# Edge loop of a graph kernel: source row buffers, the search for duplicates, and one head moved to VectorE

## The reference, cut to what matters

```python
x1 = x[edges[0]]
x2 = x[edges[1]]
e = jnp.concatenate([x1, x2], axis=1) @ Ww + bw
e = e.reshape(-1, H, 2 * HD).transpose(1, 0, 2)
e = jax.nn.leaky_relu(e, 0.01)
w = (e @ Wa + ba)[..., 0]
mat = jnp.full((H, n, n), -jnp.inf, jnp.float32)
mat = mat.at[:, edges[0], edges[1]].set(w)
mat = jax.nn.softmax(mat, axis=-1)
```

## Time and profile before

| | us |
|---|---|
| median of 3 runs | 837.27 |
| the runs' lowest and highest | 835.45, 837.58 |
| the profiled execution | 833.88 |
| its span in the trace | 832.2 |
| edge loop, from POOL's first destination gather to the last scatter's landing | 62.99 to 257.96 |

### The profile page before, as it was taken

How to read it: one execution, slowest core, us unless ns; L and a number is a source line. 1 busy time by engine, 2 the same in 40 slices (tenths; PEclk the granted TensorE clock), 3 DMA queues, 4 the chain that set the end, 5 groups by cost and what they waited for, 6 DMA issues and landing times.

```text
span 832.2 us, 9774 instructions
## 1 busy us (share of the span) xinstructions
PE 651.6 (78%) x2958; PEld 310.5 (37%) x2981; DVE 524.8 (63%) x1471; ACT 274.0 (33%) x1106; POOL 201.6 (24%) x223
## 2 busy tenths in 40 slices
PE   5972345622334929998989999989999999999997
PEld 2430112311113924455455545443434344343432
DVE  3377999989887996547473244764458745454533
ACT  2104675655661431446141010122222222222222
POOL 6047677777762000000000000011110101010100
PEclk9995556765555978999999999999999999999999
DMA  8588878788875619504000002569999999999981
GB/s 329 244 306 308 301 253 262 250 262 264 260 234 221 219 64 421 197 1 152 0 1 1 0 0 76 210 258 406 420 403 410 419 405 410 411 414 409 413 347 40
DMA packets 46648, 208.10 MB, mean 250 GB/s; under 512 B 7970, under 2 KB 12578, under 8 KB 37121
## 3 DMA queue, kind: packets, MB, share of 16 engines
q1 hardware_dynamic: 27296, 145.70, 44.1%
q0 software_dynamic: 19296, 61.75, 22.1%
HBM read 199.67 MB, written 10.31 MB: 252 GB/s over the span
## 4 chain that ended last, share of the span: by engine, by line
PE 59%; DVE 15%; DMA 9%; POOL 7%; issue 6%; ACT 2%; SPq 0%; DVEq 0%; POOLq 0%
PE bank L846 12%; PE bank L536 8%; PE bank L884 7%; PE bank L866 6%; PE bank L734 4%; PE bank L749 4%; DMA R<-tok_tab,slot_tok 3%; POOL R L447 3%; DVE R L1319 3%; POOL R L440 2%; PE bank L643 2%; PE bank L650 2%; DVE R L1323 2%; DMA score<-late,e_i 2%; PE bank L835 2%
## 5 line engine op out<-in xcount | busy, mean ns | idle before, releaser
L985 ACT ACTIVATE R<-R 128x128 f32<-128x128 f32 x384 | 113.0, 295 | 99.4 <-DVE R L1323 99.4
L584 PE MATMUL bank<-R 128*128 128x384 bf16 x144 | 49.7, 481 | 117.3 <-DVE R L1282 117.3
L846 PE MATMUL bank<-R 128*64 128x512 f32 (+1 forms) x432 | 105.9, 598 | 1.0 <-DVE R L1712 0.5
L489 POOL DMA_INDIRECT R<-tok_tab,slot_tok x33 | 33.0, 1000 | 261.7 <-DVE slot_f L1706 216.2
L536 PE MATMUL bank<-R,late 128*128 128x512 f32 x168 | 81.2, 646 | 0.7 <-DMA R<-L_Ww 0.7
L985 ACT ACTIVATION_READ_ACCUMULATOR R<-R 128x1 f32 x384 | 71.6, 187 | 0.0
L1319 DVE TENSOR_TENSOR R<-R 128x1032 f32<-128x1032 f32 x48 | 59.0, 1230 | 16.8 <-DMA R<-tab_src,e_i 9.2
L584 PEld LDWEIGHTS bank<-R 128*128 128x128 bf16 x144 | 13.4, 119 | 148.9 <-DVE R L1282 139.8
L1718 DVE TENSOR_TENSOR R<-R,bank 128x256 f32<-128x256 f32 x34 | 14.3, 420 | 86.7 <-ACT R L1098 86.7
L884 PE MATMUL bank<-R 128*128 128x512 bf16 x275 | 66.4, 380 | 2.5 <-issue 1.9
L478 POOL MEMSET R<- 128x512 f32 x3 | 1.6, 524 | 242.2 <-DVEq L1637 242.1
(11 more groups left out here) (376 smaller groups left out, 1133.8 us busy)
## 6 DMA issues: line engine op xcount, KB each, us to landing
R<-L_w SPq DMA_DIRECT2D x54, 1536.0 KB, 11.3
late<-L_w SPq DMA_DIRECT2D x18, 1536.0 KB, 10.2
R<-L_w SPq DMA_DIRECT2D x2, 3072.0 KB, 15.3
score<-R POOLq DMA_DIRECT2D x9, 512.0 KB, 12.5
R<-L_Ww SPq DMA_DIRECT2D x2, 2048.0 KB, 13.0
R<-L_W SPq DMA_DIRECT2D x4, 1024.0 KB, 9.0
R<-score SPq DMA_DIRECT2D x2, 1536.0 KB, 10.9
tab_src<-R SPq DMA_DIRECT2D x3, 516.0 KB, 2.7
```

The source lines that it names most:

```text
L584: last = pe.matmul(pb[s][:, 0:N], oh[:, e % 2, 0, P * s:P * s + P], oh[:, e % 2, 1, :], start=(e == 0), stop=(e == ET - 1))
L846: last = pe.matmul(pb[4 + i % 2][part, :], xeT[i % 2][:, k, part], w13[e % NWB][:, k, :], start=(k == 0), stop=(k == KD - 1), tile_positio ...
L985: act_.activation(own, own, ACT.Copy, accum_out=w_e3[:, t, h:h + 1]).then_inc(S("heads_summed"), 1)
```

## The change

1. `NGF` goes from 13 to 18. The five new buffers lie in `late0` and `late1`. Thirteen source gathers are still issued ahead of the loop (`NFRONT`); those of tiles 13 to 17 are issued in the loop at t = 0 to 4 and wait for no add, and from tile 18 on (t = 14) the loop gathers the source row of t+4 as before.
2. The search for duplicates compares each tile with the tile before it and with nothing else: one instruction of 128 values for each tile, none for tile 0. `tri` is gone. A duplicate inside one tile is written twice, with the same score.
3. In every odd tile VectorE's ReLU covers seven heads (896 values), and a further VectorE instruction takes ReLU, product and sum of the eighth head in one (128 values), straight to the score. ScalarE sums seven heads there.

```diff
-NGF = 13
+NGF = 18
+NFRONT = 13
...
+        def act_heads(t):
+            return H - 1 if t % 2 == 1 else H
...
-            for t in range(NEARLY, NGF):
+            for t in range(NEARLY, NFRONT):
                 gather_src(t)
             for t in range(ET):
                 if t + 4 < ET:
                     gather_dst(t + 4)
+                if NFRONT + t < NGF:
+                    gather_src(NFRONT + t)
                 if NGF <= t + 4 < ET:
                     gather_src(t + 4)
...
-                for h in range(H):
+                for h in range(act_heads(t)):
...
-                        lo = P * (j - 1) if j else 0
-                        go(stt(dup_scr[:, 256 * j:256 * j + P * (j + 1) - lo], keys[:, lo:P * (j + 1)], key_f[:, e:e + 1],
-                               before_s[:, 0:2 * P] if j else tri, ALU.is_equal, ALU.mult, accum_out=dup_f[:, e:e + 1]))
-                    if g:
-                        go(stt(dup_scr[:, P:2 * P], pb[7 - g % 2][:, 3 * P:4 * P], key_f[:, t:t + 1], ones,
-                               ALU.is_equal, ALU.mult, accum_out=dup0_f[:, g:g + 1]))
-                        settle()
-                        go(tt(dup_f[:, t:t + 1], dup_f[:, t:t + 1], dup0_f[:, g:g + 1], ALU.add))
+                        if e == 0:
+                            go(dve.memset(dup_f[:, 0:1], 0.0))
+                        else:
+                            before = keys[:, P * (j - 1):P * j] if j else pb[7 - g % 2][:, 3 * P:4 * P]
+                            go(stt(dup_scr[:, P * j:P * j + P], before, key_f[:, e:e + 1], ones, ALU.is_equal, ALU.mult,
+                                   accum_out=dup_f[:, e:e + 1]))
...
-                    dve.wait_ge(S("heads_summed"), H * (t - 1))
-                stt(prod[t % 2].rearrange(heads, h=H), ga[j][:, 0:2 * D].rearrange(heads, h=H), 0.0, bc(waR[:, None, :], [P, H, P]),
-                    ALU.max, ALU.mult).then_inc(S("prod_ready"), 1)
+                    dve.wait_ge(S("heads_summed"), heads_before(t - 1))
+                n = act_heads(t)
+                stt(prod[t % 2][:, 0:P * n].rearrange(heads, h=n), ga[j][:, 0:P * n].rearrange(heads, h=n), 0.0,
+                    bc(waR[:, None, :], [P, n, P]), ALU.max, ALU.mult).then_inc(S("prod_ready"), 1)
+                settle()
+                if n < H:
+                    go(stt(prod[t % 2][:, P * n:P * H], ga[j][:, P * n:P * H], 0.0, waR, ALU.max, ALU.mult,
+                           accum_out=w_e3[:, t, n:H]))
```

More of the change, by code:

```diff
@@ L104, in build, with heads_before @@
         onesb = sb("onesb", P, bf16)
-        before_s = sb("before_s", 2 * P)
-        ones, tri = before_s[:, 0:P], before_s[:, P:2 * P]
+        ones = sb("ones", P)[:, :]
+        def act_heads(t):
+            return H - 1 if t % 2 == 1 else H
+        def heads_before(t):
+            return sum(act_heads(e) for e in range(t))
         trib = sb("trib", P, bf16)
@@ L142, in build @@
         ab = [R2[:, 2560 + ROW * j:2560 + ROW * j + ROW] for j in range(NT)]
-        ga = [r1(10240 + ROW * j, ROW) for j in range(7)] + [R2[:, 12288 + ROW * j:12288 + ROW * j + ROW] for j in range(6)]
+        ga = ([r1(10240 + ROW * j, ROW) for j in range(7)] + [R2[:, 12288 + ROW * j:12288 + ROW * j + ROW] for j in range(6)]
+              + [late[0][:, ROW * j:ROW * j + ROW] for j in range(3)] + [late[1][:, ROW * j:ROW * j + ROW] for j in range(2)])
         gd = [r1(ROW * j, ROW) for j in range(NGD)]
@@ L393, in _ @@
             step(pool.memset(ones[:, :], 1.0))
-            step(pool.affine_select(out=tri[:, :], in_=ones[:, :], compare_op=ALU.is_gt, fill=0.0, base=0,
-                                    pattern=[[-1, P]], channel_multiplier=1))
             step(pool.affine_select(out=trib[:, :], in_=ones[:, :], compare_op=ALU.is_gt, fill=0.0, base=0,
```

5 lines of the change are left out of this document (3 added, 2 removed).

## The result

Over 20 runs of each kernel the changed kernel takes 843.28 us in the median (838.0 to 851.28) and the kernel before 836.4 us (833.73 to 839.07). The ratio is 1.0083, with a 95% interval of 1.0064 to 1.0102. The change makes the kernel slower by 6.9 us, and the interval does not reach 1.

What follows compares the result with a forecast made beforehand. POOL's DMA issue was taken to bound the edge loop. Profiled 833.9 us + 6.7 for 29 longer rounds, other terms 0, gave 840.6; 3.4 for the step to the median gave 844.0, range 833.5 to 850.

Steps and rivals of the forecast that it cites:

- The rule of the hold: Edge loop: a POOL DMA starting inside VectorE's add ends 0.83 us after the add, a scatter 0.90.
- The spacing and the search: Adds across a duplicate search come 4.45 us apart instead of 5.20, so searches push into the heavy state.
- The price: 29 edge-loop rounds, half all-heavy (+16.2 us) and half all-light (-3.2): 4.32 us a round, +6.7 us.
- the steps: Edge-loop arithmetic: C is a round's length; the add starts x = 5.6 - C after the next source gather's start.
- heavy state: Edge-loop rounds with x below 1.24: the scatter is held by the add; round 4.65 us, x = 0.95.
- light: Edge-loop rounds with x above 1.24: scatter runs free, destination gather waits for the add; round 3.98 us, x = 1.62.
- rival 1: The light state holds after searches, x staying above 1.24: faster, 832 us; chance 0.18 together with rival 4.
- The start: Moved source gathers fill POOL's wait before the third scatter but lengthen the DMA queue: taken as 0, -2.6 to +3 us.
- ScalarE and the odd head: ScalarE's 24 saved head sums lie in its idle time: 0; VectorE's net +0.14 us in 24 tiles is hidden by POOL.
- rival 2: The edge loop's mixture of states stays as before: same time, 837 us, between 835 and 839; chance 0.20.
- rival 3: All edge-loop rounds in the heavy state: slower by 16 us, 853; chance 0.08.
- rival 4: VectorE is the bound after all, so its saved 6.4 us are gained: 831 us; chance 0.18 together with rival 1.

Runs made afterwards that it cites:

- e4: The changed kernel with three idle 128-value comparisons added to each search: 838.35 us, against 836.10 for the kernel before on the same chip.
- e6: The changed kernel with VectorE's add split into two instructions of 512 and 520 values: 850.64 us, 15.1 above the kernel before.
- e5: The changed kernel with one idle 128-value comparison added to each search: 846.32 us, against 835.57 for the kernel before on the same chip.
- e1: The kernel before with the shorter search for duplicates alone: 842.48 us against 836.10; one more execution, traced on another chip, took 852.44.
- e3: The kernel before with the eighteen source row buffers and moved source gathers alone: 836.17 us against 836.10.
- e2: The kernel before with the last head of every odd tile on VectorE alone: 834.68 us against 836.10.
- e8: The changed kernel with the second operand of adds and ReLU products read from PSUM, scores not computed in full: 822.07 us, 13.5 below the kernel before.
- e11: The e9 kernel with the destination row copied to PSUM by TensorE instead of ScalarE: 852.8 us against 832.4 for the kernel before.
- e9: The changed kernel, whole result, with ScalarE copying the destination row to PSUM and VectorE adding there: 863.25 us against 849.34 for the kernel before.

## Why the prediction was right

**The time.** Forecast 844.0, slower by 6.7; measured 843.28, slower by 6.9. That the two lie 0.2 us apart is luck, as the paragraph on the price says; the direction and the mechanism are not.

**What bounds the loop.** POOL's issue, as forecast. The chain across the parts of the change holds too: VectorE's and ScalarE's savings bought nothing, and e4 shows that handing work back to VectorE helps.

**The rule of the hold.** Forecast: the DMA ends 0.83 us behind the add's end, a scatter 0.90. In the trace after, the gathers that began inside an add ended 0.81 to 0.84 us behind it and the scatters 0.90 (one 0.87); only those that began in its last 0.13 us had nothing left to wait for. One scatter that began together with an add (at 146.35 us) was not held. The prediction left open whether a product can hold too. It can: a scatter that began 0.53 us into a product of the changed kernel, at 102.74 us, took 1.60 us and ended 0.90 us behind the product. It seldom does here, because a held DMA keeps the next one out of the product; e6 shows what it costs when that is gone. The new 128-value product, which the prediction named as a danger, holds too, but it is short: 0.4 us in the 29 rounds.

**The spacing and the search.** 4.45 forecast, 4.46 measured. Its two parts were each off by about 0.07 and cancel: the odd head adds 0.08 us to a tile (1.22 against 1.14 from the product's start to the next instruction) and not 0.14, so the search saves 0.82 and not 0.89. That the search pushes the pair in, and doesn't push it out, is what the run of seven heavy rounds and the kernels e4 and e5 show.

**The price.** 4.32 us a round forecast, (252.42 - 127.58) / 29 = 4.305 measured. This number was the softest: "half of each" was chosen, not derived. Twelve of 29 scatters held is near that half, but six of them are over 1.7 us, where the prediction said many, and the spread of the changed kernel's runs (838.0 to 851.28) and e1's two traces (7 and 18 held) point to a share that changes by chance from execution to execution. e1 shows the limit of the steps, too. With its 4.31 us they give x = 1.62 + 4.31 - 3.98 = 1.95, C = 4.32 and x = 1.28, just above the 1.24 of the heavy state: by the bare numbers it would stay light, and rival 1 named 4.35 as the point. It lost 6.4 us. A margin of 0.04 us is nothing against landings that go from 5.1 to 6.8 us; the steps say in which direction a spacing pushes, not on which side a near case falls.

**The start.** Forecast: 0, from -2.6 to +3, adds of tiles 5 to 8 late. The adds of the changed kernel stand at 88.87 us and on:

```profile
88.87 1.24 DVE L1325 TENSOR_TENSOR R<-R 128x1032 f32<-128x1032 f32 x1 [1.05 <-DMA R<-tab_dst,e_i]
92.79 1.23 DVE L1325 TENSOR_TENSOR R<-R 128x1032 f32<-128x1032 f32 x1 [0.80 <-DMA R<-tab_dst,e_i]
96.52 1.23 DVE L1325 TENSOR_TENSOR R<-R 128x1032 f32<-128x1032 f32 x1 [0.71 <-DMA R<-tab_dst,e_i]
100.95 1.23 DVE L1325 TENSOR_TENSOR R<-R 128x1032 f32<-128x1032 f32 x1
```

Before, they stood at 85.09, 88.03, 90.97 and 96.17. They are 3.8 to 5.6 us late, 1.95 of it from ahead of the loop, and they now wait for destination rows, which the moved source gathers queue ahead of. The third scatter, at 87.09 before, stands at 95.88, and the wait before it is 3.63 us, for VectorE, where it was 2.88: the 2.6 us that were the best case were not gained there. (The prediction called that wait the only one; two more, of 1.06 and 0.77 us, followed it before.) By the source gather of tile 18 only 1.5 us of the delay are left, and e3 puts the part at 0 within 2.2 us. The sign of the term can't be told; its size is inside the bounds.

**ScalarE and the odd head.** 0 forecast; e2 measured -1.4, within its interval.

**The rivals.** The light state that holds (rival 1) and the mixture as before (rival 2) fall with the 12 held scatters and the interval above 1.0064. Heavy throughout (rival 3) is not reached, though e5 comes near with +10.75. VectorE as the bound (rival 4) falls with e4. The rule of the Trainium skill (SBUF — State Buffer, section "Who interferes with whom") on two SBUF inputs fits what was measured: with one of them in PSUM the hold is gone (e8). The inference in the same section, that writing descriptors isn't stalled by `tensor_tensor`, can't be carried over to these gathers and scatters, whose row numbers lie in SBUF; by it the rounds would take 3.82 us. Which part of such a DMA waits, the reading or the writing, no run here tells.

## What to carry to other kernels

Before costing a change by how much work it takes from an engine, look at which instructions of other engines begin inside its long ones, and whether a landing time locks the two engines in step: in such a loop a shorter step can land in a worse place, and the time need not follow the work even in direction. A cheap test is idle work of two sizes in the step; a time that goes up with the one and down with the other shows a lock and not a bound. And a stall that is shortened or removed pays only up to what stands next: the following instruction that can hold in the same way, or the engine that must make a copy to avoid it.

## What the runs showed of the hardware

- An indirect DMA of POOL that begins while VectorE works on an add or product with two SBUF operands ends 0.81 to 0.84 us (a scatter 0.90 us) after that instruction, and takes up to 2.07 us instead of 1.02. With the second operand in PSUM there is no delay (1.02 us, begun 0.66 us into the add), and the add itself stays at 1.22 to 1.23 us.
- The hold works the other way as well where the two begin together. In the traces here no scatter or destination gather that began up to 0.04 us into such an instruction was held; VectorE's instruction was longer instead (e1: the scatter at 200.25 us took 1.03 us, and the add at 200.20 took 1.31 instead of 1.23). Two source gathers that began 0.01 us into an add (e3 at 153.86, e4 at 155.10) were held, 2.02 us each.
- What counts is the instruction in which the DMA begins. One that began in the first of two halves was not held by the second, though that followed without a gap (150.79 to 151.88 us in e6); and the release can let the next DMA start inside the next such instruction.
- In e11 the granted TensorE clock was 0.90 in the mean from 120 to 280 us, where the kernel before had 0.57 from 120 to 257 us. The copies brought TensorE from 53 us busy in 137 us to 112 in 160; e9, whose copies are ScalarE's, had 0.55 in the mean from 60 to 270 us. No gain of the loop by the clock shows: TensorE's copies waited 35.3 us for VectorE's products from 120 to 250 us.
